# Attention stacks by way of DRAM, ternary weights by ScalarE's sign, and another order in the head of a cross-attention and BitNet layer

## The reference

```python
q, k, v = proj(Wq, layernorm(x)), proj(Wk, ctx), proj(Wv, ctx)      # (32, 128, 512)
q, k = rope(q, 8), rope(k, 8)                                        # per head: 512 x 16
p = softmax(q @ k.T / sqrt(16)); x = x + proj(Wo, p @ v)
weight_quant(w) = clip(round(w / mean|w|), -1, 1) * mean|w|
act_quant(x)    = clip(round(x * 128 / max|x|), -128, 127) / (128 / max|x|)   # per row
gate, up = act_quant(layernorm(x)) @ weight_quant(w_gate).T, ... w_up
x = x + act_quant(fwht(silu(gate) * up)) @ weight_quant(w_down).T
```

## Time and profile before

| | |
|---|---|
| median of 3 runs | 1619.53 us (1617.6 to 1630.68) |
| the profiled execution | 1624.36 us, its span 1622.6 us |
| PE busy | 1481.5 us, 91% of the span |
| DVE busy | 1318.3 us, 81% |
| ACT busy | 1125.9 us, 69% |
| POOL busy | 848.4 us, 52% |
| DMA | 79750 packets, 99.50 MB, mean 61 GB/s |

### The profile page before, as it was taken

The page is one execution under the profiler, slowest core; times in us unless marked ns, Lnnn a source line. Parts: engine busy times, 40 slices in busy tenths (PEclk is TensorE's granted clock), DMA queues, the critical chain, the costliest instruction groups (busy, mean ns, idle before and its releaser), DMA issues.

```text
span 1622.6 us, 26340 instructions
## 1 busy us (share of the span) xinstructions
PE 1481.5 (91%) x8579; PEld 666.8 (41%) x8674; DVE 1318.3 (81%) x2317; ACT 1125.9 (69%) x1841; POOL 848.4 (52%) x648
## 2 busy tenths in 40 slices
PE   1378999999999999999999999999999999999984
PEld 0112344444444444444444434444444444444433
DVE  4477988888888888888888888888888888888741
ACT  4436677777777777777777777777777777777662
POOL 0111665555556655555556655555566555555464
PEclk9568999999999999999999999999999999999997
DMA  5633312233333233223332322323332322333000
GB/s 195 167 111 59 56 44 56 54 57 57 66 66 64 42 59 59 55 56 62 66 66 46 60 56 55 58 56 66 66 64 42 63 53 56 57 50 53 14 7 14
DMA packets 79750, 99.50 MB, mean 61 GB/s; under 512 B 9472, under 2 KB 59904, under 8 KB 78592
## 3 DMA queue, kind: packets, MB, share of 16 engines
q1 hardware_dynamic: 79056, 93.62, 30.1%
q10 hardware_dynamic: 560, 4.19, 0.7%
HBM read 38.80 MB, written 8.39 MB: 29 GB/s over the span
## 4 chain that ended last, share of the span: by engine, by line
PE 75%; DVE 12%; issue 3%; POOL 3%; ACT 2%; DMA 2%; SPq 1%; POOLq 0%; DVEq 0%; ACTq 0%
PE pv L468 15%; PE s L453 14%; PE ring L498 13%; PE s L425 12%; PE ring L543 6%; PE ring L397 6%; PE ring L519 4%; DVE maxima L989 3%; PE ring L477 2%; PE ring L530 2%; DVE h_res L1020 1%; DVE st L1022 1%; DVE attn L1009 1%; DVE turned_pv L999 1%; POOL region L1222 1%
## 5 line engine op out<-in xcount | busy, mean ns | idle before, releaser
L989 DVE TENSOR_REDUCE maxima<-s 128x1 bf16<-128x512 f32 x1024 | 667.0, 683 | 119.9 <-PE s L425 117.8
L688 ACT ACTIVATE region<-s 128x512 f32<-128x512 f32 x1024 | 575.2, 597 | 208.1 <-PE s L453 167.4
L1221 POOL TENSOR_TENSOR region<-region 128x512 f32<-128x512 f32 x192 | 253.3, 1319 | 391.3 <-DVE region L1069 363.8
L425 PE MATMUL s<-region 96*128 96x512 bf16 x1024 | 374.0, 390 | 26.0 <-DMA region<-parts 15.8
L453 PE MATMUL s<-region 97*128 97x512 bf16 x1024 | 352.8, 384 | 5.5 <-ACT region L688 3.0
L468 PE MATMUL pv<-region,v_ext 128*32 128x512 f32 x2048 | 267.2, 605 | 0.5 <-DVE turned_pv L999 0.4
L1222 POOL TENSOR_TENSOR region<-region 128x512 f32<-128x512 f32 x192 | 245.4, 1278 | 0.0
L453 PEld LDWEIGHTS s<-region 97*128 97x128 bf16 x1024 | 95.9, 98 | 240.0 <-ACT region L688 121.2
L425 PEld LDWEIGHTS s<-region 96*128 96x128 bf16 x1024 | 97.6, 97 | 205.8 <-DVE maxima L989 74.7
L1256 POOL TENSOR_TENSOR region<-region,parts 128x1024 f32<-128x1024 f32 x32 | 68.1, 2129 | 175.1 <-ACT parts L755 175.1
L704 ACT ACTIVATE region<-ring 128x512 f32<-128x512 f32 x128 | 76.2, 596 | 116.1 <-PE ring L509 116.1
(11 more groups left out here) (113 smaller groups left out, 1858.1 us busy)
## 6 DMA issues: line engine op xcount, KB each, us to landing
region<-parts SPq DMA_DIRECT2D x768, 64.0 KB
x_in<-in_x SPq DMA_DIRECT2D x32, 256.0 KB, 2.6
c_in<-in_ctx SPq DMA_DIRECT2D x32, 256.0 KB, 2.9
x_res<-in_x SPq DMA_DIRECT2D x32, 256.0 KB, 4.0
out<-o_sb SPq DMA_DIRECT2D x32, 256.0 KB, 4.1
region<-in_wg_t ACTq DMA_DIRECT2D x1, 2048.0 KB, 10.6
region<-in_wu_t SPq DMA_DIRECT2D x1, 2048.0 KB, 7.4
region<-in_wd_t SPq DMA_DIRECT2D x1, 2048.0 KB, 14.8
```

The lines of the kernel that those rows point to most:

```text
L425: pe.matmul(s1[p][:, :], q_stack[k][0:STACK, h, 128 * c:128 * (c + 1)], k_stack[k][0:STACK, h, :], start=True, stop=True).then_inc(s1_full ...
L688: act.activation(probs[:, n % 8, :], s2[n % 2][:, :], ACT.Exp, scale=SCALE).then_inc(exp_done, 1)
L989: dve.reduce_max(maxima[:, c, h:h + 1], s1[p][:, :], AXX).then_inc(s1_max[p], 1)
L1221: pool.tensor_tensor(o[:, :, 0, :], a[:, :, 0, :], a[:, :, 1, :], ALU.add)
```

## The change

**Stacks.** The parts are first written to a scratch tensor in DRAM, 2 transfers for each part (`write_part`), and read back into the stacks, 2 for each part (`read_part`): 12 transfers in place of 24. The terms change places so that equal ones are neighbours, and a read may fill two of them from one source by a broadcast. `read_part` waits on SP's queue until the writes have landed; the writes of batch b wait for the reads of batch b-1. `first_part` and `second_part` now wait for the writes of the batch before in place of the whole stack.

**Weights.** VectorE rounds (scale, then the constant, one pass), and ScalarE's Sign of the rounded value less the constant gives -1, 0 or 1: one pass on each engine in place of one on ScalarE and two on VectorE. The up weights are staged in regions that later hold `probs`, the rope results and the third stack slots, so they can be loaded without waiting for gate; the first `exps` and the use of slot 2 wait for their signs. All weight loads are on ScalarE's queue.

**Order.** The steps are cut at another place (LAST is B + 5, the ring begins with yT0). Batch 0's projections and parts stand ahead of the weight pieces on ScalarE. The late constants go first on SP's queue. `third_part` on GpSimd follows the second half of the Hadamard transform directly. Some scores, maxima, glu and y pieces change places by a few positions.

```diff
-Q_TERMS = (0, 0, 1, 1, 0, 2)
-K_TERMS = (0, 1, 0, 1, 2, 0)
+Q_TERMS = (0, 0, 1, 1, 2, 0)
+K_TERMS = (0, 1, 0, 1, 0, 2)
...
+        scratch = nc.dram_tensor("scratch", (2, 2, 3, 2, ROPE, NH, T), BF16).ap()
...
+            if i == 1:
+                if n * j < 4096:
+                    return region[2][:, n * j:n * (j + 1)]
+                return region[n * j // 2048 - 1][:, 6144:8192]
...
-            def stack_part(b, part):
-                sp.wait_ge((part1, part2, part3)[part], b + 1)
-                if part == 0:
-                    wait(sp, s2_full, 32 * (b - 2))
-                for w, (terms, dst) in enumerate(((Q_TERMS, q_stack[k]), (K_TERMS, k_stack[k]))):
-                    for r in range(len(terms)):
-                        if terms[r] == part:
-                            for half in range(2):
-                                row = DH * r + ROPE * half
-                                sp.dma_start(dst[row:row + ROPE, :, :], parts[64 * w:64 * (w + 1), part, half, :]) \
-                                  .then_inc(stacked, 16)
+            def write_part(b, part):
+                sp.wait_ge((part1, part2, part3)[part], b + 1)
+                if part == 0:
+                    wait(sp, stacked, 16 * READS * b)
+                for w in range(2):
+                    sp.dma_start(scratch[b % 2, w, part].rearrange("a d h n -> (d h) a n"),
+                                 parts[64 * w:64 * (w + 1), part, :, :]).then_inc(written[part], 16)
+            def read_part(b, part):
+                for i in range(part + 1):
+                    sp.wait_ge(written[i], 32 * (b + 1))
+                if part == 0:
+                    wait(sp, s2_full, 32 * (b - 2))
+                    unstaged(sp, b)
+                q, key = (scratch[b % 2, w].rearrange("t a d h n -> t (a d) (h n)") for w in range(2))
+                twice = [2, DH, NH * T]
+                if part == 0:
+                    rows = ((q_stack[k], 0, 32, q[0:1].to_broadcast(twice)), (q_stack[k], 80, 96, q[0]))
+                elif part == 1:
+                    both = key[0:2].rearrange("t r n -> (t r) n").unsqueeze(0).to_broadcast([2, 2 * DH, NH * T])
+                    rows = ((q_stack[k], 32, 64, q[1:2].to_broadcast(twice)), (k_stack[k], 0, 64, both))
+                else:
+                    rows = ((q_stack[k], 64, 80, q[2]), (k_stack[k], 64, 96, key[0:3:2]))
+                for dst, lo, hi, src in rows:
+                    sp.dma_start(dst[lo:hi, :, :], src).then_inc(stacked, 16)
...
             def step(t):            # SP
-                stack_part(t + 1, 1)
-                stack_part(t + 1, 2)
-                stack_max(t)
-                load_consts(t + 2)
...
+                write_part(t, 1)
+                read_part(t, 0)
+                read_part(t, 1)
+                write_part(t, 2)
+                load_late_consts(t + 1)
+                read_part(t, 2)
+                load_residual(t - 1)
+                stack_max(t - 1)
+                store(t - 4)
+                load_consts(t + 1)
+                load(t + 2)
+                write_part(t + 1, 0)
...
-            def round_piece(b, i, j):            # ScalarE
-                act.activation(w, w, ACT.Copy, bias=ROUND, scale=w_inv[:, i:i + 1]).then_inc(w_rounded, 1)
+            def sign_piece(b, i, j):
+                act.wait_ge(w_rounded, UPTO[i] + j + 1)
+                act.activation(piece(i, j, flat(weights[i])), staged(i, j), ACT.Sign, bias=round_neg[:, :])                    .then_inc(ternary, 1)
             def exps(b, n):
+                if n == b == 0:
+                    act.wait_ge(ternary, UPTO[1] + 2)
...
-            def clip_piece(b, i, j):            # VectorE
-                dve.tensor_scalar(w, w, ROUND - 1, ROUND + 1, ALU.max, ALU.min).then_inc(clipped, 1)
-                dve.tensor_scalar(piece(i, j, flat(weights[i])), w, ROUND, None, ALU.subtract).then_inc(ternary, 1)
+            def round_piece(b, i, j):
+                dve.tensor_scalar(w, w, w_inv[:, i:i + 1], ROUND, ALU.mult, ALU.add).then_inc(w_rounded, 1)
...
             def step(t):            # GpSimd
                 mix(t - 2, 0)
-                third_part(t)
+                hadamard_last(t - 3, 0)
+                rstd1(t + 1)
                 mix(t - 2, 1)
                 hadamard_last(t - 3, 1)
-                rstd1(t + 1)
                 rstd2(t - 2)
                 hadamard_half(t - 2, 0)
                 rest(t + 1)
                 hadamard_half(t - 2, 1)
-                hadamard_last(t - 2, 0)
+                third_part(t + 1)
```

More of the change, by code:

```diff
@@ L20 @@
 SCALE = float(DH) ** -0.5
-Q_TERMS = (0, 0, 1, 1, 0, 2)
-K_TERMS = (0, 1, 0, 1, 2, 0)
+Q_TERMS = (0, 0, 1, 1, 2, 0)
+K_TERMS = (0, 1, 0, 1, 0, 2)
 STACK = len(Q_TERMS) * DH
[L26 to L32, removed]
+READS = 6
+RING = {"yT0": 3, "yT1": 3, "down": 3, "zT0": 2, "v": -1, "zT1": 2, "wo": 1, "y0": 2, "zT2": 2, "y1": 2, "mT": 0,
+        "zT3": 2, "y2": 2, "y3": 2, "xqT": 1, "gate0": 1, "up0": 1, "gate1": 1, "up1": 1, "gate2": 1, "up2": 1,
+        "gate3": 1, "up3": 1, "rope": -2, "turn": -2, "pass": -2}
 NRING = 3
@@ L211, in layer @@
         part1, rest_done, part2, part3 = sem("part1"), sem("rest_done"), sem("part2"), sem("part3")
-        stacked = sem("stacked")
+        written, stacked = [sem(f"written{i}") for i in range(3)], sem("stacked")
         s1_full, s1_max = [sem(f"s1_full{i}") for i in range(2)], [sem(f"s1_max{i}") for i in range(2)]
@@ L254, in load_half, with unstaged @@
             v = src.rearrange("(c p) n -> p c n", p=128)
[L255 to L261, removed]
+            cut = lambda t, m: t.rearrange("p (c n) -> p c n", c=m)
+            if h == 0:
+                dst = region[2][:, 0:4096] if i == 1 else region[1][:, 0:4096]
+                engine.dma_start(cut(dst, n // 2), v[:, 0:n // 2, :]).then_inc(w_in[i][0], 16)
+                return
+            third, last = (region[1][:, 6144:8192], region[2][:, 6144:8192]) if i == 1 else (region[1][:, 4096:6144], y_last[:, :])
+            engine.dma_start(cut(third, n // 4), v[:, n // 2:3 * n // 4, :]).then_inc(w_in[i][1], 16)
+            engine.dma_start(cut(last, n // 4), v[:, 3 * n // 4:n, :]).then_inc(w_in[i][1], 16)
+        def unstaged(engine, b):
+            if b == 2:
+                engine.wait_ge(ternary, UPTO[2])
         @block.sync
@@ L547, in step @@
             def step(t):
-                score_max(t, 9)
+                weigh(t - 1, 2)
+                scores(t - 1, 16)
+                y_transpose(t - 3, 0)
+                score_max(t, 10)
                 scores(t - 1, 17)
-                score_max(t, 10)
                 weigh(t - 1, 3)
@@ L751, in first_part @@
                     return
-                wait(act, stacked, 16 * STACK_DMAS * b)
+                wait(act, written[0], 32 * b)
                 moved(act, "pass", b)
@@ L759, in second_part @@
                     return
+                wait(act, written[1], 32 * b)
                 act.wait_ge(rest_done, b + 1)
@@ L1260, in third_part @@
                     return
+                wait(pool, written[2], 32 * b)
                 pool.wait_ge(part2, b + 1)
```

249 lines of the change are left out of this document (123 added, 126 removed).

## The result

| | before | after |
|---|---|---|
| median time, us | 1621.1 | 2363.8 (2358.2 to 2367.2) |
| ratio to before | | 1.457 [1.449, 1.464] |
| span of the profiled execution, us | 1622.6 | 2363.8 |
| mean granted clock of TensorE | 0.97 | 0.83 |
| first score_max, batch 0 / last batch, us | 69.18 / 1489.06 | 79.15 / 2225.00 |

The change makes the kernel slower by 742 us. The forecast was 2138 us, with 2045 to 2280 for the likeliest case and 1602 to 2280 for eight in ten. The direction and the mechanism (narrow reads on two engines, a wait in each batch) are right; the size is 226 us short and 84 us above the upper end.

A forecast was written before the change was run, and what follows sets the result against it. It took TensorE's rate to bound the steady state, with waits in the head. After the change: first reader 70.4, 31 loops of 62.5 (1937.5) and 133.5 sum to 2141.4 of span, so 2138 us predicted, range 1602 to 2280.

The forecast's parts named there:

- outermost 2 at the source, two engines: Four of the six reads from DRAM: each carried by two DMA engines, TensorE waiting 15.6 us per batch; chance 0.55.
- T in batch 0: T is the moment a batch's second part ends; in batch 0 it was forecast at 36.3 us.
- the first projection: Start of batch 0's projections, held only by the constants: taken as 25 us, bounds 22 and 31.
- Sign loads no further table: ScalarE's Sign was costed like Copy; a rival with 16 engines had two table loads per sign group, 31 us, about 1634.
- the first reader: Batch 0's first score_max, which reads the stacks: forecast at 70.4 us, against 69.2 before.
- the loop: From one batch's first score_max to the next: 27.4 + 34.1 + 1.0 for the clock, 62.5 us, 31 times.
- the row price of 0.325 us: Time of one DMA engine per 8 KB row of the narrow reads, taken from the weight load; range 0.30 to 0.35.
- the tail: From the last batch's first score_max to the kernel's end: 133.5 us, as in the profile before.
- The rival of 16 engines: All 16 engines share every read, nothing waits, the head gains 17 us: 1602.5 us; sixteen-engine cases together had chance 0.37.
- The rival of the swallowed gain: Head's gain lost to constants (31 for 25) and batch 0's exponentials waiting for up weights' signs: 1614.5 us; no separate chance.
- confined, but less: Two engines run faster, or the third write is not behind the reads: 52 to 56 us a batch, 1810 to 1940; chance 0.08.
- the order of the steps: Rotation of the steps, order of single scores and round_y: costed at nothing, bounds +/- 0.3 us a batch.

The follow-up runs named there:

- the plain variant: Changed kernel with every narrow read (outermost dimension 2) cut into plain ones, 10 reads in place of 6, still by way of DRAM: 1622.3 us, ratio 1.0003.

## Why the prediction was right and wrong

- **Right: outermost 2 at the source, two engines.** Share 0.12 for over 20 us of each batch, as forecast (0.13). The Trainium skill, "DMA: Bandwidth & Descriptors", section on why a DMA increments its semaphore by 16, has this rule; the trace agrees for an outermost 2 (0.12), and the run with rows outermost agrees for 16 (share 1.08 and 1.11). One addition comes from the runs: an outermost 2 contiguous with what follows counts together with it.
- **Right: T in batch 0**, 36.8 for 36.3, and the first projection at 25.26 for 25; the 25 was a choice between bounds of 22 and 31, so this close it is luck. Sign loads no further table: there is one load of 1.28 us in the whole execution, and a sign pass takes 1.99 us.
- **Wrong by 8.7 us, once: the first reader**, 79.15 for 70.4. The sum had the reads of batch 0 alone on the engines; the second half of the up weights (2 MB, issued at 48.50) was served between their rows and took most of the engines from 49 to 56 (shares of 0.68 to 1.02).
- **Wrong by 6.7 us, 31 times: the loop.** That is 208 of the 222 us between the sum of 2141.4 and the span of 2363.8. In the batch shown, 70.1 us, the terms are: T at 29.2 for 27.4 + 1.0 of clock, so 0.8 more; the issue of the last reads at T + 31.6 for T + 26.2, so 5.4 more, of which the 32 key rows at 0.5 in place of 0.325 are 32 x 0.175 = 5.6; and the last read 9.4 for 7.9, 1.5 more, while x_res, output and inputs share the engines with it (0.78 and 227 GB/s at 1175). This batch is 0.9 us longer than the mean of 69.2. The step that failed is the row price of 0.325 us. Taken from a load of rows to 128 partitions, it held for q's rows (0.33), but not for the key's 32 rows twice, where two engines that run in step hold each other up and the mean was 0.5. The range let it go to 0.35 only, so its upper end of 2280 rested on a bound for this price that no row of before showed for such a read.
- **Wrong by 5.3 us, once: the tail**, 138.8 for 133.5. In the plain variant it is 133.4 (1620.2 - 1486.8). All of it is lost before the tail's first Hadamard product of 16 matmuls, which comes 47.3 us after score_max here (2272.31) and 41.9 there (1528.64): after the last wait TensorE has a clock of 0.50 for 5 us and 0.68 over 10, in which it gets 37 matmuls done, not 52 as in the plain variant at 1.00. That the clock is the whole reason is likely, not tested.
- **The rival of 16 engines (1602.5)** was too low by some 9 us in its best form. Its terms add up to 52.5 and a gain of 16.4 us, not 52.7 and 17, so it should have read 1603.1. Its places in time were right once the down weights were out of the way (score_max near 49, measured 52.8; exponential near 91, measured 91.4), but the lead at the exponential was 16 us, at batch 1's Hadamard product 13.6, at the end 12.5 by the spans and 9.1 by the medians. The change's own order holds the exponential behind batch 1's stacks and these behind the down weights. The rival of the swallowed gain named the exponentials' wait for signs, but not what made the signs late.
- **The rival "confined, but less"** gave 52 to 56 us a batch for a third write that is not behind the reads. With these writes on ScalarE's queue a batch still takes 66.2 us (2270.0).
- **Put at nothing: the order of the steps.** With the direct transfers it makes the kernel 0.7% slower (1634.5), with plain reads it costs nothing that shows (1622.3). In the kernel after it is hidden by the waits.

## What to carry to other kernels

Count for every DMA what its outermost dimension is on both sides after contiguous dimensions are joined, and put the long dimension outside a broadcast, not inside. A transfer that two engines carry delays everything queued behind it, so price it by rows per engine and look at the next dependent write in the same queue. In this head a start won was lost again while large loads ran beside the next batch's small transfers, so look at those when you place a load.

## What the runs showed of the hardware

- q's two reads with an outermost broadcast of 2 moved 49 GB/s, and with the key's last read they kept the kernel at 2009 us; with rows outermost and that read plain it took 1616.
- Rows of 8 KB on two engines took 0.31 to 0.33 us each where the two copies were written 16 partitions apart. Where they were 32 apart, 33 of 64 packets took 0.6 us, most of them while the two engines ran close together, and the mean was 0.5 (the batch from 1110); other DRAM addresses, another matrix and another place in the queue didn't change it, and two reads of 16 rows an engine, written 16 apart, didn't have it. The distance alone was not tested.
- Two writes of 128 KB in SyncE's queue behind such reads landed 26 us after their issue; the same writes from ScalarE's queue had a median of 6.4 us.
- In the batch shown the granted clock of TensorE fell from 1.00 (2.4 GHz) to 0.50 (1.2 GHz) while it waited, and was 0.50 still at 1181 with TensorE busy; at the start of the tail it was 0.68 over the first 10 us.
